# Two neighbouring products of a stencil made by one VectorE instruction, in five of ten steps

## The chip, the cores and the metric

The kernel runs on one core of a Trainium2 chip. The metric is the device time of one execution in microseconds (us); the median of three runs is given. A profile of one execution comes with it: when each instruction ran on each engine, what it waited for, and the clock that TensorE was granted.

## The reference, cut to what matters

Two layers are computed on an image batch of 8 x 32 x 32 pixels (H and W) and 64 channels. The second (a ternary 3x3 convolution) comes after the part that is changed. The first normalises the input, computes coefficient fields from convolutions and Sobel filters, and then takes five steps of a recurrence:

```python
K = 5
cm_x, cp_x = (-Ax + 2.0 * Bx, Ax + 2.0 * Bx)
cm_y, cp_y = (-Ay + 2.0 * By, Ay + 2.0 * By)
for _ in range(K):
    prev = h
    h = D * (c0 * h0 - 2.0 * E * h
             + cm_x * jnp.roll(h, 1, axis=2) + cp_x * jnp.roll(h, -1, axis=2)
             + cm_y * jnp.roll(h, 1, axis=3) + cp_y * jnp.roll(h, -1, axis=3))
    h = h + D * (2.0 * DT) * fsrc
    h0 = prev
```

Axis 2 is the position w in a row, axis 3 is the channel. So each step needs five products of a coefficient field with the present state (two of it shifted by one row position, two by one channel, one not shifted), one product with the state before it, and a source term.

## The kernel before, in words

The batch is cut into two tiles t = 0 and 1 of four images. A tile is 128 partitions (32 image rows by 4 images) by 2048 columns (32 positions w by 64 channels), all fp32. The five steps of the two tiles run interleaved: `ORDER` at line 38 is (0,0), (1,0), (0,1), (2,0), (1,1), (3,0), (2,1), (4,0), (3,1), (4,1), each a pair (k, t) of step and tile. Below, "step (2,0)" means step k = 2 of tile 0.

`coef` holds seven coefficient fields of each tile, 2048 columns each; A0, AE, FS, AXM, AXP, AYM and AYP are their numbers (AYM is 2 and AYP is 5). `state` holds for each tile two copies of h with a border of one position and one channel around it, so that a shifted h is a view that begins elsewhere (`h_at`).

One step (k, t) is this work:

- VectorE (`step`, lines 978 to 1005, and `multiply`, lines 906 to 919) makes the five products in the order AYP, AXP, AE, AXM, AYM. Each is one instruction of 2048 columns, and each writes one of three slots of a buffer `ring` in turn. A product may start when the slot's former content has been summed: the semaphore wait in `wait_summed` asks for all products up to the third last one. `product` is counted up by one at its end.
- In the five steps (1,0), (2,0), (1,1), (3,0) and (2,1) VectorE then makes a sixth product of the same length, A0 times h, into `first_two` (line 1004), which is kept for the tile's next step. GpSimd's queue then adds the source to it by an accumulating DMA (line 350).
- TensorE (`add_source`, `back_to_natural`, `add_products`, the loop at line 1306) sums in PSUM. Each summand takes 16 transposing matmuls of 128 x 128 (line 1180). For a step it first sums the kept product of that tile, then turns the state of the step before back to natural layout (line 1087, 16 matmuls), then sums the five products as they come. So 7 groups of 16 matmuls belong to a step.
- ScalarE (line 380) copies the finished sum from PSUM, copies what TensorE turned back into `state`, and fills the border (four small copies). The next step of the same tile waits for that border. Between two steps of one tile there is a step of the other tile, except for (1,0), which comes right behind (0,0), and (4,1), right behind (3,1).

The order on each engine is the order of the code; there is no scheduler. VectorE makes the last coefficient fields of tile 1 between step (0,0) and step (1,0).

Of the kernel before, what the change touches and what calls it, by code (L numbers as in the profile page):

```python
# [9 lines left out]

# [1 line left out]

# [1 line left out]

B, H, W, C = 8, 32, 32, 64
TILES = 2
# [8 lines left out]
STEPS = 5  # L25
# [8 lines left out]
A0, AE, FS, AXM, AXP, AYM, AYP = 1, 6, 0, 3, 4, 2, 5  # L34
RING = 3
# [39 lines left out]
def network(nc, x, wide_taps, norms, matrices, out_cols, conv_w, out):  # L75
    f32, f32r, i32 = mybir.dt.float32, mybir.dt.float32r, mybir.dt.int32
    ALU, ACT, AX = mybir.AluOpType, mybir.ActivationFunctionType, mybir.AxisListType

    jobs = job_table()
    job_no = {name: i for i, (name, _) in enumerate(jobs)}  # L80
    slot_of = dict(jobs)
    uses_before, seen = {}, [0] * SLOTS
# [4 lines left out]
    with ExitStack() as ctx:  # L87
        def sb(name, shape, dt=f32):
            return ctx.enter_context(nc.sbuf_tensor(name, shape, dt))

        def sem(name):
            return ctx.enter_context(nc.semaphore(name))


        coef = sb("coef", [128, TILES, NCOEF, N])
        state = sb("state", [128, TILES, 2, ROWS, PITCH])
        ring = sb("ring", [128, RING, N])
# [57 lines left out]
        def h_at(t, k, dw=0, dc=0, w0=0, w1=W):  # L155

            return state[:, t, k % 2, 1 + dw + w0:1 + dw + w1, 1 + dc:1 + dc + C]
# [7 lines left out]
        def wc(ap):  # L165
            return ap.rearrange("p (w c) -> p w c", c=C)

        def half(ap, h):
            return ap[:, h * HALF:(h + 1) * HALF]
# [8 lines left out]
        def part(ap, t, i):  # L178
            return ap[:, out_cuts[t][i]:out_cuts[t][i + 1]]
# [16 lines left out]
        def slot_ap(name):  # L196
            return psum[:, slot_of[name], :]
# [17 lines left out]
        newton_ready, axp_ready, ayp_ready = sem("newton_ready"), sem("axp_ready"), sem("ayp_ready")  # L215
# [3 lines left out]
        ax_full, ay_full = ([sem(f"{n}{t}") for t in range(TILES)] for n in ("ax_full", "ay_full"))  # L219
# [7 lines left out]
        product, ring_free = sem("product"), sem("ring_free")  # L227
# [11 lines left out]
        def wait_job(eng, name):  # L239

            eng.wait_ge(pe_job, job_no[name] + 1)

        def wait_reader(eng, name):

            eng.wait_ge(slot_free[slot_of[name]], uses_before[name] + 1)

        def frees(ins, name):
            ins.then_inc(slot_free[slot_of[name]], 1)

        def kept(k, t):  # L250

            return k > 1 and (k, t) != ORDER[-1]
# [9 lines left out]
        def states_through(k, t):  # L262

            return sum(kk < STEPS - 1 for kk, _ in ORDER[:ORDER.index((k, t)) + 1])
# [365 lines left out]
        def _(dve):  # L630
            steps, asked = [0], [0]
            V = nc.vector
# [262 lines left out]
            made = [0]  # L895
            sum_ends = {products_through(k, t): (k, t) for k in range(STEPS) for t in range(TILES)}

            def wait_summed(n):

                if n in sum_ends:  # L900
                    k, t = sum_ends[n]
                    wait_job(dve, f"acc_{k}_{t}_1")
                else:
                    dve.wait_ge(ring_free, n - sum(end < n for end in sum_ends))

            def multiply(t, k, a, dw, dc):

                slot = made[0] % RING
                if made[0] < 2:
                    wait_job(dve, "t2_1_1")  # L910
                    dve.wait_ge(ayp_ready, 1)
                    dve.wait_ge(ae_ready, 1)
                if made[0] == 2:
                    dve.wait_ge(dense_m_ready, 6)
                if made[0] >= RING:
                    wait_summed(made[0] - RING + 1)
                made[0] += 1
                V.tensor_tensor(wc(ring[:, slot, :]), wc(coef[:, t, a, :]), h_at(t, k, dw, dc), ALU.mult)\  # L918
                    .then_inc(product, 1)

            def residual(t):

                for h in range(2):
                    wait_reader(dve, f"acc_{STEPS - 1}_{t}_{h}")
                    wait_job(dve, f"tx_{t}_{h}")
                    frees(V.tensor_tensor(half(coef[:, t, 2, :], h), slot_ap(f"tx_{t}_{h}"),
                                          half(coef[:, t, 0, :], h), ALU.add), f"tx_{t}_{h}")
                    wait_reader(dve, f"tx_{t}_{h}")
                    x1 = half(coef[:, t, 2, :], h).rearrange("p (j h b) -> p j h b", b=BT, h=H)
                    for b in range(0, BT, 2):  # L930
                        V.bn_stats(stats[:, t, h, b:b + 2, :].rearrange("p b s -> p (b s)"), x1[:, :, :, b:b + 2])\
                            .then_inc(mv_ready, 1)
# [40 lines left out]
            def output_sum(t, h):  # L973
                wait_reader(dve, f"cf_{t}_{h}")
                V.tensor_tensor(part(coef[:, t, 3, :], t, h), part(coef[:, t, 0, :], t, h),  # L975
                                part(coef[:, t, 2, :], t, h), ALU.add).then_inc(sum_ready, 1)

            def step(k, t, then_do=()):

                def then(i):  # L980
                    for at, what in then_do:
                        if at == i:
                            what()

                if k > 1 and not kept(k, t):
                    multiply(t, k + 1, A0, 0, 0)
                then(-1)
                if k == 0:
                    dve.wait_ge(s_halo, 4 * (t + 1))
                else:  # L990
                    dve.wait_ge(halo_ready, 4 * states_through(k - 1, t))
                for i, (a, dw, dc) in enumerate(((AYP, 0, 1), (AXP, 1, 0), (AE, 0, 0), (AXM, -1, 0), (AYM, 0, -1))):
                    if k == 0 and i == 0:
                        dve.wait_ge(ayp_ready, t + 1)
                        dve.wait_ge(axp_ready, t + 1)
                    if k == 0 and a == AXM:
                        dve.wait_ge(ax_full[t], 16)
                    if k == 0 and a == AYM:
                        dve.wait_ge(ay_full[t], 16)
                    multiply(t, k, a, dw, dc)  # L1000
                    then(i)
                if k and k + 1 < STEPS and kept(k + 1, t):
                    dve.wait_ge(kept_free[t], k)
                    V.tensor_tensor(wc(first_two[t][:, :]), wc(coef[:, t, A0, :]), h_at(t, k), ALU.mult)\  # L1004
                        .then_inc(kept_made[t], 1)
# [37 lines left out]
            then(V.tensor_tensor(outw[:, 1:2], outw[:, 2:3], outp[:, 2:3], ALU.mult))  # L1043
            signal(V.tensor_tensor(outw[:, 3:4], outp[:, 1:2], outw[:, 1:2], ALU.add), outw_ready, 1)
            step(0, 0)
            over_rows(1)
            over_channels(1)
            divergence_taken()
            source(1)
            step(1, 0)  # L1050
            for k, t in ORDER[2:-1]:
                step(k, t)
            residual(0)
            step(STEPS - 1, 1, ((-1, lambda: spread(0)), (0, lambda: ask_norm(0)), (1, lambda: second_norm(0)),
                                  (3, lambda: normalise(0))))
            lower_half(0, 0)
            lower_half(0, 1)
            residual(1)
            spread(1)
            ask_norm(1)  # L1060
# [350 lines left out]
```

## Time and profile before

| what | us |
|---|---|
| median of three runs (lowest, highest) | 279.26 (278.02, 279.52) |
| the profiled execution, device time | 277.91 |
| its span, from first to last instruction | 276.1 |
| TensorE busy | 233.6 (85% of the span) |
| VectorE busy | 247.2 (90%) |
| ScalarE busy | 133.8 (48%) |

The profiled execution took 1.35 us less than the median of the three runs. In a row of a timeline the first number is the start in us from the begin of the span, the second how long the group took, then engine, line, operation, what was written and read, the count (x5), and in brackets how long the engine had been idle before and which engine ended that. PE is TensorE, PEld its weight loads, DVE VectorE, ACT ScalarE, POOL GpSimd.

### The profile page before, as it was taken

What the parts mean: (1) busy time and instruction counts of PE and PEld (TensorE: products, weight loads), DVE (VectorE), ACT (ScalarE), POOL (GpSimd) and SP (SyncE); (2) the same over time, 40 slices, a digit from 0 to 9 for tenths busy, and PEclk for the clock granted to TensorE, in tenths of its full rate; (3) what the DMA queues carried; (4) which work ended last, traced back from release to release, by engine and by line L of the source; (5) the groups of instructions that cost most, each with busy time, mean ns of one, the idle gap of its engine ahead of it and who ended that gap; (6) DMA issues with size and microseconds to landing.
All of it is one profiled execution on the core that took longest, in us unless ns stands there. A gap on an engine that the chain in (4) does not pass through costs nothing.

```text
span 276.1 us, 5235 instructions
## 1 busy us (share of the span) xinstructions
PE 233.6 (85%) x2276; PEld 209.6 (76%) x2276; DVE 247.2 (90%) x196; ACT 133.8 (48%) x207; POOL 16.8 (6%) x36
## 2 busy tenths in 40 slices
PE   0137999999959999279999999999999987889793
PEld 0136889989925588279989999898989986767683
DVE  3799999999999989999998999999999989886821
ACT  3294776879860054702623425160603246917743
POOL 2000000003310201101000101010101000000000
PEclk9999999999979999959999999999999999999999
DMA  6950000005998771990700334248610030000124
GB/s 213 350 116 0 0 4 6 2 0 112 199 205 253 152 152 38 209 209 2 154 0 2 76 78 94 61 116 190 129 26 1 0 138 17 2 0 0 62 93 152
DMA packets 7190, 24.94 MB, mean 90 GB/s; under 512 B 2816, under 2 KB 3328, under 8 KB 5120
## 3 DMA queue, kind: packets, MB, share of 16 engines
q0 software_dynamic: 2304, 14.68, 26.6%
q1 hardware_dynamic: 4720, 9.61, 10.6%
q10 hardware_dynamic: 144, 0.33, 0.4%
q8 instruction: 18, 0.29, 0.4%
q14 instruction: 4, 0.03, 0.0%
HBM read 6.79 MB, written 2.10 MB: 32 GB/s over the span
## 4 chain that ended last, share of the span: by engine, by line
DVE 54%; PE 27%; issue 9%; ACT 7%; DMA 1%; DVEq 0%; ACTq 0%
DVE ring L918 24%; DVE coef L653 8%; PE psum L1180 8%; PE psum L1170 6%; ACT coef L380 5%; PE psum L1257 5%; DVE first_two L1004 4%; PE psum L1117 3%; PE psum L1087 3%; DVE state L729 2%; DVE coef L964 1%; DMA bn<-in_norms 1%; DVE ring L722 1%; DVE hi_s L734 1%; DVE gsum L687 1%
## 5 line engine op out<-in xcount | busy, mean ns | idle before, releaser
L918 DVE TENSOR_TENSOR ring<-coef,state 128x2048 f32<-128x2048 f32 x51 | 113.5, 2286 | 2.1 <-PE psum L1180 1.9
L1180 PE MATMUL psum<-mats,ring 128*128 128x128 f32 x816 | 96.6, 278 | 9.6 <-DVE ring L918 9.5
L1180 PEld LDWEIGHTS psum<-mats,ring 128*128 128x128 f32 x816 | 91.4, 144 | 13.3 <-DVE ring L918 12.9
L380 ACT ACTIVATE state<-psum 128x1024 f32<-128x1024 f32 x36 | 35.1, 1028 | 74.3 <-PE psum L1180 60.2
L653 DVE SCALAR_TENSOR_TENSOR coef<-coef 128x2048 f32<-128x2048 f32 x16 | 36.4, 2290 | 0.7 <-issue 0.2
L380 ACT ACTIVATE coef<-coef 128x2048 f32<-128x2048 f32 (+1 forms) x10 | 17.6, 1783 | 10.1 <-DMA coef<-coef 9.9
L1257 PE MATMUL psum<-hi,dense_m 128*128 128x512 f32 (+1 forms) x54 | 20.0, 379 | 0.9 <-ACT coef L380 0.9
L1139 PEld LDWEIGHTS psum<-coef,state 32*128 32x128 f32 x672 | 19.4, 187 | 1.4 <-issue 1.3
L380 ACT ACTIVATE coef<-psum 128x512 f32<-128x512 f32 (+2 forms) x23 | 17.5, 766 | 5.4 <-PE psum L1117 4.3
L1139 PE MATMUL psum<-coef,state 32*128 32x64 f32 x672 | 20.0, 271 | 0.0
L1257 PE MATMUL psum<-lo,dense_m 128*128 128x512 f32 (+1 forms) x54 | 19.5, 369 | 0.0
L1180 PE MATMUL psum<-mats,first_two 128*128 128x128 f32 x144 | 17.3, 273 | 1.8 <-issue 1.2
L1180 PEld LDWEIGHTS psum<-mats,first_two 128*128 128x128 f32 x144 | 15.9, 141 | 2.3 <-ACT state L380 1.4
L1087 PE MATMUL psum<-mats,state 128*128 128x128 f32 x128 | 15.4, 273 | 0.7 <-ACT state L380 0.7
L1087 PEld LDWEIGHTS psum<-mats,state 128*128 128x128 f32 x128 | 14.1, 141 | 1.2 <-ACT state L380 1.1
L380 ACT ACTIVATE coef<-coef,gn 64x512 f32<-64x512 f32 x9 | 11.3, 1322 | 3.4 <-DVE gn L653 3.4
L975 DVE TENSOR_TENSOR coef<-coef 128x512 f32<-128x512 f32 (+2 forms) x7 | 5.4, 767 | 8.2 <-ACT coef L380 8.1
L1117 PE MATMUL psum<-hi_s,sobel_m 128*128 128x512 f32 (+2 forms) x48 | 12.1, 391 | 0.2 <-DVE hi_s L734 0.2
L1170 PE MATMUL psum<-coef,mats 128*128 128x512 f32 (+2 forms) x20 | 9.6, 616 | 3.1 <-ACT first_two L380 3.1
L1257 PEld LDWEIGHTS psum<-hi,dense_m 128*128 128x128 f32 x54 | 10.2, 188 | 2.7 <-issue 1.1
L380 ACT ACTIVATE coef<-psum,outp,wred 128x512 f32<-128x512 f32 (+2 forms) x7 | 5.9, 838 | 13.0 <-PE psum L1257 13.0
L1270 PE MATMUL psum<-gsum,mats 128*128 128x32 f32 x4 | 1.2, 404 | 12.2 <-DVE gsum L687 12.2
(133 smaller groups left out, 280.4 us busy)
## 6 DMA issues: line engine op xcount, KB each, us to landing
first_two<-coef POOLq DMA_DIRECT2D x7, 1024.0 KB, 8.5
coef<-coef POOLq DMA_DIRECT2D x5, 1024.0 KB, 8.8
coef<-in_x SPq DMA_DIRECT2D x2, 1024.0 KB, 6.0
coef<-in_wide_taps SPq DMA_DIRECT2D x3, 384.0 KB, 7.6
ring<-in_x SPq DMA_DIRECT2D x2, 512.0 KB, 6.0
ring<-in_x SPq DMA_DIRECT2D x1, 1024.0 KB, 10.3
coef<-coef SPq DMA_DIRECT2D x1, 1024.0 KB, 7.6
out<-coef SPq DMA_DIRECT2D x2, 512.0 KB, 3.1
```

Source lines behind the costliest of these rows:

```text
L380: return nc.scalar.activation(dst, src, func, **kw)
L653: return V.scalar_tensor_tensor(out=out_ap, in0=in0, scalar=scalar, in1=in1, op0=op0, op1=op1)
L729: signal(V.tensor_tensor(s, s, root(t).unsqueeze(1).broadcast_to([128, W, C]), ALU.mult), s_ready, t + 1)
L918: V.tensor_tensor(wc(ring[:, slot, :]), wc(coef[:, t, a, :]), h_at(t, k, dw, dc), ALU.mult)\
L975: V.tensor_tensor(part(coef[:, t, 3, :], t, h), part(coef[:, t, 0, :], t, h), part(coef[:, t, 2, :], t, h), ALU.add).then_inc(sum_ready, 1)
L1004: V.tensor_tensor(wc(first_two[t][:, :]), wc(coef[:, t, A0, :]), h_at(t, k), ALU.mult)\
L1087: ins = nc.tensor.transpose(dst[:, j * 128:j * 128 + 128], src, ident)
L1117: ins = mm(dst[:, bank * BANK + to * C:bank * BANK + (to + count) * C], sobel_m[:, m, :], part[:, frm * C:(frm + count) * C], start=(i == ...
L1139: ins = mm(banks[a][:, j * 2 * W:(j + 1) * 2 * W], sT[t][p, 8 * h + j, dy * BT:dy * BT + 128], taps(8 * h + j)[p, dy, :, :].rearrange("p v ...
L1170: ins = mm(out_ap, m, src, start=(i == 0), stop=(i == len(pieces) - 1), skip_group_check=True)
L1180: ins = mm(slot_ap(name)[:, (j % 8) * 128:(j % 8) * 128 + 128], src[:, j * 128:j * 128 + 128], ident, is_transpose=True, start=first and j ...
L1257: ins = mm(to, dense_m[:, b, dy, :], rows[:, j0 + b:j1 + b, dy * BT:dy * BT + 128], start=(n == 0), stop=(n == len(steps) - 1))
```

## The change

In the five steps that keep a product, the two products of the channel direction (AYM with the state one channel lower, AYP with the state one channel higher) become one instruction of 4096 columns, and it stands first in the step. The two coefficient fields are read with a stride of three fields, the two shifted states as one view with a step of two elements between its halves, and two slots of `ring` are written: slots 0 and 1, or 1 and 2, or 2 and 0, as they come. It waits until all but the last product before it have been summed, and counts `product` up by two at its end. The other three products and the kept one follow. The other five steps are as before; their code is moved into a function of its own.

```diff
+            def multiply_both_channels(t, k):
+
+                slot = made[0] % RING
+                wait_summed(made[0] - RING + 2)
+                made[0] += 2
+                to = ring[:, slot:slot + 2, :] if slot + 2 <= RING else ring[:, 0:RING:RING - 1, :]
+                factors = coef[:, t, AYM:AYP + 1:AYP - AYM, :]
+                left = h_at(t, k, 0, -1)
+                both = bass.AP(left.tensor, left.offset, [left.ap[0], [2, 2], *left.ap[1:]])
+                V.tensor_tensor(to.rearrange("p k (w c) -> p k w c", c=C),
+                                factors.rearrange("p k (w c) -> p k w c", c=C), both, ALU.mult).then_inc(product, 2)
...
+                if k and k + 1 < STEPS and kept(k + 1, t):
+                    multiply_both_channels(t, k)
+                    for a, dw, dc in ((AXP, 1, 0), (AE, 0, 0), (AXM, -1, 0)):
+                        multiply(t, k, a, dw, dc)
+                else:
+                    single_products(t, k, then)
```

On VectorE, at steps (1,0), (0,1) and (2,0), this stands in a row before the change (`ring_free` and `pe_job` count what TensorE has summed, `halo_ready` the borders of the state, `kept_free` the reading of the kept product):

```order
L653 SCALAR_TENSOR_TENSOR coef<-coef,state 128x2048 [waits slot_free3,slot_free2]
L918 TENSOR_TENSOR ring<-coef,state 128x2048 [waits ring_free,halo_ready]
L918 TENSOR_TENSOR ring<-coef,state 128x2048 [waits ring_free]
L918 TENSOR_TENSOR ring<-coef,state 128x2048 [waits pe_job]
L918 TENSOR_TENSOR ring<-coef,state 128x2048 [waits ring_free] x2
L1004 TENSOR_TENSOR first_two0<-coef,state 128x2048 [waits kept_free0]
```

and this with the change, at the same place:

```order
L653 SCALAR_TENSOR_TENSOR coef<-coef,state 128x2048 [waits slot_free3,slot_free2]
L930 TENSOR_TENSOR ring<-coef,state 128x2x2048 [waits ring_free,halo_ready]
L918 TENSOR_TENSOR ring<-coef,state 128x2048 [waits pe_job]
L918 TENSOR_TENSOR ring<-coef,state 128x2048 [waits ring_free] x2
L1025 TENSOR_TENSOR first_two0<-coef,state 128x2048 [waits kept_free0]
```

Six instructions have become five; the first one now holds two products, and the product behind it waits for the whole sum of the step before (`pe_job`), as the third did.

On VectorE again, step (2,0) and the start of step (1,1), as a difference:

```order
-L918 TENSOR_TENSOR ring<-coef,state 128x2048 [waits ring_free,halo_ready]
-L918 TENSOR_TENSOR ring<-coef,state 128x2048 [waits ring_free]
+L930 TENSOR_TENSOR ring<-coef,state 128x4096 [waits ring_free,halo_ready]
 L918 TENSOR_TENSOR ring<-coef,state 128x2048 [waits pe_job]
 L918 TENSOR_TENSOR ring<-coef,state 128x2048 [waits ring_free] x2
-L1004 TENSOR_TENSOR first_two0<-coef,state 128x2048 [waits kept_free0]
-L918 TENSOR_TENSOR ring<-coef,state 128x2048 [waits ring_free,halo_ready]
-L918 TENSOR_TENSOR ring<-coef,state 128x2048 [waits ring_free]
+L1025 TENSOR_TENSOR first_two0<-coef,state 128x2048 [waits kept_free0]
+L930 TENSOR_TENSOR ring<-coef,state 128x2x2048 [waits ring_free,halo_ready]
```

The same happens in each of the five steps; TensorE's, ScalarE's and GpSimd's instructions keep their order.

## Rows read from the trace of the kernel before

**Rows 1.** The page: busy time by engine, and the granted clock in 40 slices
```profile
PE 233.6 (85%) x2276; PEld 209.6 (76%) x2276; DVE 247.2 (90%) x196; ACT 133.8 (48%) x207; POOL 16.8 (6%) x36
PEclk9999999999979999959999999999999999999999
```
**Rows 2.** Timeline of VectorE from 111 to 216 us
```profile
111.96 2.35 DVE L885 TENSOR_TENSOR coef<-psum,coef 128x1024 f32<-128x1024 f32 x2
114.41 2.29 DVE L653 SCALAR_TENSOR_TENSOR coef<-coef,state 128x2048 f32<-128x2048 f32 x1
116.62 11.09 DVE L918 TENSOR_TENSOR ring<-coef,state 128x2048 f32<-128x2048 f32 x5
...
148.23 4.50 DVE L918 TENSOR_TENSOR ring<-coef,state 128x2048 f32<-128x2048 f32 x2 [0.69 <-PE psum L1180]
...
154.84 11.09 DVE L918 TENSOR_TENSOR ring<-coef,state 128x2048 f32<-128x2048 f32 x5
165.85 2.28 DVE L1004 TENSOR_TENSOR first_two<-coef,state 128x2048 f32<-128x2048 f32 x1
168.06 11.09 DVE L918 TENSOR_TENSOR ring<-coef,state 128x2048 f32<-128x2048 f32 x5
```
**Rows 3.** The chain that ended last: start us, us, what; 194 to 219 us
```profile
194.57 8.69 DVE ring L918 x4
203.29 2.29 DVE ring L918
205.63 7.20 PE psum L1180 x64
212.84 1.75 PE psum L1087 x16
214.58 4.38 PE psum L1180 x40
218.99 1.03 ACT state L380
```
**Rows 4.** VectorE durations, ns least/median/greatest of a line; then two timeline rows of shorter ones
```profile
L918 DVE TENSOR_TENSOR ring<-coef,state x51: 2274/2285/2295, 90.6 to 236.6; 128x2048 f32<-128x2048 f32 x51
L722 DVE TENSOR_TENSOR ring<-state,gsum x2: 2292/2294/2295, 19.9 to 37.9; 128x2048 f32<-128x2048 f32 x2
255.53 1.23 DVE L975 TENSOR_TENSOR coef<-coef 128x1024 f32<-128x1024 f32 x1
...
264.37 0.69 DVE L975 TENSOR_TENSOR coef<-coef 128x512 f32<-128x512 f32 x1 [2.08 <-ACT coef L380]
```
**Rows 5.** Timeline of TensorE from 78 to 180 us
```profile
79.20 3.62 PE L1170 MATMUL psum<-coef,mats 128*128 128x512 f32 x6 [3.12 <-ACT first_two L380]
...
111.46 1.94 PE L1180 MATMUL psum<-mats,first_two 128*128 128x128 f32 x16 [1.17 <-issue]
118.96 11.09 PE L1180 MATMUL psum<-mats,ring 128*128 128x128 f32 x80 [5.57 <-DVE ring L918]
129.89 1.91 PE L1180 MATMUL psum<-mats,first_two 128*128 128x128 f32 x16
...
133.38 7.37 PE L1180 MATMUL psum<-mats,ring 128*128 128x128 f32 x64
140.99 1.97 PE L1180 MATMUL psum<-mats,ring 128*128 128x128 f32 x16 [0.23 <-DVE ring L918]
...
146.28 8.90 PE L1180 MATMUL psum<-mats,ring 128*128 128x128 f32 x80
155.01 1.91 PE L1180 MATMUL psum<-mats,first_two 128*128 128x128 f32 x16
156.76 1.91 PE L1087 MATMUL psum<-mats,state 128*128 128x128 f32 x16
158.51 7.25 PE L1180 MATMUL psum<-mats,ring 128*128 128x128 f32 x64
165.99 1.97 PE L1180 MATMUL psum<-mats,ring 128*128 128x128 f32 x16 [0.24 <-DVE ring L918]
167.79 1.91 PE L1180 MATMUL psum<-mats,first_two 128*128 128x128 f32 x16
```
**Rows 6.** Windows: from:to us, length, PE busy (matmuls), granted clock, DMA share, GB/s
```profile
79.00:79.50 0.50, 0.30 (x1) 0.51 0.96 190
82.00:82.50 0.50, 0.50 (x2) 0.57 0.95 186
82.50:83.00 0.50, 0.50 (x4) 1.00 0.97 198
...
116.00:116.50 0.50, 0.00 (x0) 1.00 1.20 246
116.50:117.00 0.50, 0.00 (x0) 0.56 0.95 197
...
123.00:123.50 0.50, 0.50 (x5) 0.61 1.20 246
```
**Rows 7.** The stretch 150 to 205 us: ScalarE's border copies before step (2,1)
```profile
172.65 0.71 ACT L380 ACTIVATE state<-state 128x64 f32<-128x64 f32 x4
181.27 11.09 DVE L918 TENSOR_TENSOR ring<-coef,state 128x2048 f32<-128x2048 f32 x5
```

More of the change, by code:

```diff
@@ L11 @@
 from contextlib import ExitStack
-from concourse import mybir
+from concourse import bass, mybir
 B, H, W, C = 8, 32, 32, 64
@@ L976, in output_sum, with single_products @@
                                 part(coef[:, t, 2, :], t, h), ALU.add).then_inc(sum_ready, 1)
+            def single_products(t, k, then):
+                for i, (a, dw, dc) in enumerate(((AYP, 0, 1), (AXP, 1, 0), (AE, 0, 0), (AXM, -1, 0), (AYM, 0, -1))):
+                    if k == 0 and i == 0:
+                        dve.wait_ge(ayp_ready, t + 1)
+                        dve.wait_ge(axp_ready, t + 1)
+                    if k == 0 and a == AXM:
+                        dve.wait_ge(ax_full[t], 16)
+                    if k == 0 and a == AYM:
+                        dve.wait_ge(ay_full[t], 16)
+                    multiply(t, k, a, dw, dc)
+                    then(i)
             def step(k, t, then_do=()):
@@ L991, in step @@
                     dve.wait_ge(halo_ready, 4 * states_through(k - 1, t))
[L992 to L1001, printed above, removed]
+                if k and k + 1 < STEPS and kept(k + 1, t):
+                    multiply_both_channels(t, k)
+                    for a, dw, dc in ((AXP, 1, 0), (AE, 0, 0), (AXM, -1, 0)):
+                        multiply(t, k, a, dw, dc)
+                else:
+                    single_products(t, k, then)
                 if k and k + 1 < STEPS and kept(k + 1, t):
```

## The prediction

> **What bounds the kernel now.** I read the page first: VectorE and TensorE are both busy nearly all the time [rows 1], so neither share says which one sets the end. The timeline of VectorE says it for the stretch that is changed. From 154.84 us on, steps follow each other with no idle time: 154.84 to 168.06 is 13.22 us for six instructions of 2048 columns, 2.20 us from start to start [rows 2]. TensorE has seven groups of 16 matmuls in the same step. A group takes 156.76 - 155.01 = 1.75 us, seven take 12.25, and it waits about 1 us in a step for a product [rows 5]. So VectorE bounds here, with TensorE close behind. The chain that ended last agrees: it runs along VectorE's products up to 205.6 us, and along TensorE from there [rows 3]. All of what happens between 116 and 205 us therefore arrives at the end one for one.
>
> Ahead of 154.84 the roles are different. VectorE waits once, 0.69 us, at 148.23 [rows 2]: the fourth product of step (2,0) needs the slot of the first, and TensorE began to sum that one only at 146.28 [rows 5]. TensorE is late there because of what happened at 118.96. It had been idle for 5.57 us, until the first product of step (1,0) was done [rows 5]. The granted clock had fallen from full (2.4 GHz) to half (1.2 GHz) between 116.5 and 117 and came back to full at about 123.4 [rows 6], the one dip that the page shows there [rows 1]. The 80 matmuls of the step took 129.89 - 118.96 = 10.93 us, against 155.01 - 146.28 = 8.73 us for the 80 of step (2,0) at full clock: 2.20 us lost. That fits half of the 4.4 us between the restart and the return of the clock. No product was missing meanwhile: the fifth was done at 116.62 + 11.09 = 127.71. So from 118.96 to 138.6 TensorE is the one that everything hangs on.
>
> **What the change saves on VectorE.** A 2048-column product takes 2.285 us and starts 2.20 us after the one before, since its start overlaps the other's end by 0.08 [rows 2, 4]. The 4096-column instruction is not in the trace. By the slope between 512 columns (0.69) and 2048 (2.285), 1.038 ns a column, it takes 2.285 + 2.13 = 4.41; by the slope from 1024 columns (1.23), 1.030 ns, 4.395. I take 4.41, the longer base line. From start to start that is 4.33 against 4.405 for two: 0.07 us saved in a step. The bounds: two full durations (4.57, a loss of 0.09), and 4.395 (a gain of 0.09). The pattern, three levels and a view that overlaps itself, should not slow it: a product with broadcast and regrouped operands at L722 takes 2.294 [rows 4]. In five steps 0.35, if all counted; those of (1,0) and (2,0) lie before the wait for TensorE at 148.23, which swallows them. Three are left: 0.21 us (bounds -0.27 and 0.27).
>
> A rule bears on this size. The trace shows successive products 2.20 us apart although each lasts 2.285. The Trainium skill, "VectorE: DVE Perf Modes", section "The TRN2 errata", gives fp32 tensor_tensor of N columns as (N + 151) / 0.96 ns and says that small tiles pay the fixed part each. By it two products cost 4.58 and the long one 4.42, 0.16 us a step, an estimate from that page; over three steps the saving would be 0.47 instead of 0.21 and the forecast 0.26 us lower. The trace speaks against counting it so, since most of the fixed part is overlapped.
>
> **What the change costs at step (1,0).** The first product no longer ends after 2.3 us but only with the second. The instruction starts at 116.62 as before, as the instructions ahead of it are untouched [rows 2]; it ends at 121.03 and TensorE restarts at 121.08 (0.05 us after, as at 118.96), 2.12 us later. The clock has fallen by then, at 116.5 to 117, before either restart [rows 6]. The question is when it comes back. The trace has two restarts at half clock: at 79.20 us it was back at 82.4, 3.2 us after; at 118.96 at 123.4, 4.4 us after [rows 5, 6]. I take the middle, 3.8 us, so a loss of 1.9. The 80 matmuls then end at 121.08 + 8.73 + 1.90 = 131.71, against 129.89: 1.82 us later. The later products are there in time (the fifth at 116.62 + 4.33 + 3 x 2.20 + 0.08 = 127.63), so nothing else delays it.
>
> How much of the 1.82 arrives: in step (0,1) TensorE waits for products. From 133.38 four sums of 1.75 would end at 140.36, the fifth begins at 140.99 [rows 5]: 0.63 us of slack. Behind it there is none up to 146.28. So the first sum of step (2,0) begins 1.82 - 0.63 = 1.19 us later, at 147.47, and VectorE's fourth product, which waits for it, starts 1.19 later as well, at 149.42. From there VectorE runs without a wait. The long instruction of step (2,0) itself is hidden: it starts once the fourth sum of (0,1) is done, some 142.4, and ends at 146.8, before TensorE asks for it.
>
> The Trainium skill, "TensorE: Matmul & The Clock Gate", section "What's actually happening", says that the throttled state is the default and that activity releases it. The fall during the idle stretch and the return after the restart agree with it [rows 5, 6]; it gives no reason that the return should stay at 123.4.
>
> **The later four steps.** In steps (1,1), (3,0) and (2,1) TensorE gets its first product at T + 4.46 (T being the step's start on VectorE) where it would be ready at about T + 3.6 (158.51 - 154.84 = 3.67). It idles some 0.8 us, but then has two products at once. Its seven groups (12.25) fit into VectorE's 13.15. The tightest wait is that of VectorE's product behind the pair and one more: free at T + 4.33 + 2.20 = 6.53, and it needs the first sum, which is done 1.95 us after its start (148.23 - 146.28 [rows 2, 5]), at T + 6.41. Margin 0.12 us, so I count nothing; the next one has 0.6. The finished sum comes at about T + 13.2, some 0.25 later than now; the border for the tile's next step was there at 173.36 for a step that begins at 181.27 [rows 7], 7.9 us of cover.
>
> **The sum.** Cost 1.19, saving 0.21: 0.98, say 1.0 us slower. Against the profiled execution (277.91) that is 278.9. The median of the runs shown is 1.35 us above that execution, so the expected median is 279.26 + 1.0 = 280.3 us, slower by 0.36%.
>
> **The rivals.** (a) The clock comes back no later than before, at 123.4. The loss is then (123.4 - 121.08) / 2 = 1.16, TensorE ends 121.08 + 8.73 + 1.16 = 130.97, 1.08 late; 0.45 arrives, less 0.21: 0.24 us slower, 279.5. For it speaks that the second restart's return took longer than the first's, so the return isn't a fixed time after the restart. Chance 0.2. (b) On the other side: the half clock doesn't matter, because the clock is full again soon after the restart or hasn't fallen. Full at the restart, the matmuls end at 121.08 + 8.73 = 129.81, earlier than now. The saving stands in four steps, 0.28 us: 279.0, faster. The cost is below the saving when TensorE ends less than 0.63 + 0.28 = 0.9 us late, that is with a loss under 1.0, when the clock is back within 2.0 us; neither restart in the trace shows that. Chance 0.1. (c) The return takes longer, or the 0.12 us of margin is not there. If the clock returns 5.5 us after the restart, TensorE ends 0.85 later than forecast: +1.8 us. If the fourth product waits 0.3 us in each of three steps (the bound is TensorE's present slack of 1 us a step, less what it must wait), +0.9 as well: 281.2. For it speaks that TensorE stands idle 7.7 us instead of 5.57, and has work for 12.25 of the 13.15 us of a step; against it, that 1.95 us is one measured number and the other rows give the same 0.05 from product to sum. Chance 0.15. The forecast has 0.55.
>
> **How the numbers follow.** 0.5% is 1.4 us, about what a measurement of this kernel can tell from no change. The forecast's own range, with returns of 3.2 and 4.4 us (losses 1.6 and 2.2: 0.7 and 1.3 us) and the bounds of the long instruction, is +0.5 to +1.6. The range over all takes in (a) and most of (b) and (c): -0.2 to +2.2, and some 0.4 for where a median falls in runs that lie 1.5 us apart: 278.7 to 281.8. Slower by over 0.5% takes most of (c) and a fifth of the forecast: 0.26. Faster by over 0.5% is no case here, only scatter: 0.03. The rest, 0.71, is within.
>
> **What would show it.** In the profile after: the long instruction at 4.41 us, and 13.15 us per step; TensorE's restart at 121.1, half clock behind it for over 2.5 us, and the 80 matmuls of step (1,0) ending near 131.7; VectorE's wait at step (2,0) grown, with its next step (1,1) starting near 156.0 instead of 154.84. I am wrong if VectorE starts step (1,1) at or before 154.9, if the long instruction takes over 4.6, or if VectorE waits in steps (1,1) to (2,1).

## The result, and the profile after

| | median us | lowest, highest | runs |
|---|---|---|---|
| before | 278.62 | 277.82, 279.52 | 17 |
| after | 279.90 | 279.27, 280.62 | 17 |

The changed kernel takes 1.0047 times the time of the one before (95% interval 1.0033 to 1.0060), 1.3 us more. The forecast was 1.0 us more. With more runs the median of before lies 0.64 us lower than the three runs gave, so the absolute time came out at 279.9 and not at 280.3.

The profiled execution of after took 280.57 us, its span 278.8. The page's lines that answer to [rows 1]:

```profile
PE 233.2 (84%) x2276; PEld 209.6 (75%) x2276; DVE 247.0 (89%) x191; ACT 133.9 (48%) x207; POOL 16.8 (6%) x36
...
PEclk9999999999969999959999999999999999999999
```

The busy times are those of before to within 0.4 us; VectorE has five instructions fewer. So the difference is idle time. The timeline of VectorE after the change, in the same columns as [rows 2]:

```profile
115.69 2.29 DVE L653 SCALAR_TENSOR_TENSOR coef<-coef,state 128x2048 f32<-128x2048 f32 x1
117.90 4.42 DVE L930 TENSOR_TENSOR ring<-coef,state 128x4096 f32<-128x4096 f32 x1
122.23 2.28 DVE L918 TENSOR_TENSOR ring<-coef,state 128x2048 f32<-128x2048 f32 x1
126.08 4.50 DVE L918 TENSOR_TENSOR ring<-coef,state 128x2048 f32<-128x2048 f32 x2 [1.57 <-PE psum L1201]
130.49 2.29 DVE L1025 TENSOR_TENSOR first_two<-coef,state 128x2048 f32<-128x2048 f32 x1
132.69 11.10 DVE L918 TENSOR_TENSOR ring<-coef,state 128x2048 f32<-128x2048 f32 x5
143.74 4.43 DVE L930 TENSOR_TENSOR ring<-coef,state 128x4096 f32<-128x4096 f32 x1
148.08 2.29 DVE L918 TENSOR_TENSOR ring<-coef,state 128x2048 f32<-128x2048 f32 x1
151.09 4.50 DVE L918 TENSOR_TENSOR ring<-coef,state 128x2048 f32<-128x2048 f32 x2 [0.72 <-PE psum L1201]
...
157.70 4.42 DVE L930 TENSOR_TENSOR ring<-coef,state 128x4096 f32<-128x4096 f32 x1
...
197.14 22.11 DVE L918 TENSOR_TENSOR ring<-coef,state 128x2048 f32<-128x2048 f32 x10
```

The reader is to see three stretches here:

- **Up to the start of step (1,0)**, 117.90 against 116.62 [rows 2]: 1.28 us later, and nothing in it was changed. TensorE's clock was at half until 85.0 us here (the window below), and until 82.4 in the execution of before [rows 6]. This is scatter between executions: in nine profiles that run the same code up to here, the start of step (1,0) follows that return of the clock (shown with the experiment that fills an earlier gap).
- **From (1,0) to (1,1)**: 157.70 - 117.90 = 39.80 us, against 154.84 - 116.62 = 38.22 before. This is the cost, 1.58 us. VectorE waits 1.57 us at the fourth product of step (1,0), where it did not wait before. The wait at step (2,0) is what it was (0.72 for 0.69).
- **From (1,1) to (4,0)**, three steps: 197.14 - 157.70 = 39.44 us. Before, step (4,0) began at 194.49 (the next timeline), so 39.65: 0.21 us are saved, as forecast.

```profile
194.49 22.10 DVE L918 TENSOR_TENSOR ring<-coef,state 128x2048 f32<-128x2048 f32 x10
```

1.28 + 1.58 - 0.21 = 2.65, the 2.7 us between the two spans. TensorE in the same stretch, timeline first, then windows in the columns of [rows 6]:

```profile
111.87 1.94 PE L1201 MATMUL psum<-mats,first_two 128*128 128x128 f32 x16 [1.16 <-issue]
122.37 10.68 PE L1201 MATMUL psum<-mats,ring 128*128 128x128 f32 x80 [8.56 <-DVE ring L930]
132.88 1.91 PE L1201 MATMUL psum<-mats,first_two 128*128 128x128 f32 x16
...
162.18 8.95 PE L1201 MATMUL psum<-mats,ring 128*128 128x128 f32 x80 [0.65 <-DVE ring L930]
```
```profile
119.00:119.50 0.50, 0.00 (x0) 0.62 0.56 115
...
125.50:126.00 0.50, 0.50 (x4) 0.55 0.12 16
84.50:85.00 0.50, 0.50 (x4) 0.51 0.71 147
```

TensorE restarts 4.47 us after VectorE began the step (122.37), with the clock at half, and the clock is full again at about 125.95, 3.6 us later. The chain that ended last shows how that gets back to VectorE:

```profile
117.90 4.43 DVE ring L930
122.32 0.04 issue
122.37 3.69 PE psum L1201 x16
126.06 0.02 issue
126.08 1.80 DVE ring L918
```

The first sum (the 16 matmuls of the first product) takes 3.69 us at half clock; at full clock it is 1.95, with its last matmul's latency (148.23 - 146.28 [rows 2, 5]). VectorE's fourth product writes the ring slot that this sum reads, and can't start before the sum has ended.

### The profile page after: what moved, and what is told of

Its sections match the earlier page's. It is cut to its first block, busy times and chain, and to the rows that moved or that the text cites. A ratio compares the mean times of both kernels' runs of the same rounds, so it can differ in the third digit from the quotient of the medians.

```text
span 278.8 us, 5230 instructions
## 1 busy us (share of the span) xinstructions
PE 233.2 (84%) x2276; PEld 209.6 (75%) x2276; DVE 247.0 (89%) x191; ACT 133.9 (48%) x207; POOL 16.8 (6%) x36
## 4 chain that ended last, share of the span: by engine, by line
DVE 56%; PE 28%; issue 10%; ACT 4%; DMA 1%; DVEq 0%; ACTq 0%
DVE ring L918 20%; PE psum L1201 10%; DVE coef L653 8%; PE psum L1191 7%; DVE ring L930 6%; PE psum L1278 5%; PE psum L1108 3%; DVE first_two L1025 2%; PE psum L1138 2%; ACT coef L380 2%; DVE coef L976 2%; DVE lo_s L737 2%; DVE state L729 2%; DMA bn<-in_norms 1%; DVE ring L722 1%
## 5 line engine op out<-in xcount | busy, mean ns | idle before, releaser
L1201 PE MATMUL psum<-mats,ring 128*128 128x128 f32 x816 | 94.8, 276 | 13.2 <-DVE ring L930 10.6
L918 DVE TENSOR_TENSOR ring<-coef,state 128x2048 f32<-128x2048 f32 x41 | 91.7, 2287 | 4.9 <-PE psum L1201 4.7
L930 DVE TENSOR_TENSOR ring<-coef,state 128x4096 f32<-128x4096 f32 x5 | 22.1, 4420 | 0.0
```

The lines of the kernel that those rows point to most:

```text
L930: V.tensor_tensor(to.rearrange("p k (w c) -> p k w c", c=C), factors.rearrange("p k (w c) -> p k w c", c=C), both, ALU.mult).then_inc(prod ...
L1201: ins = mm(slot_ap(name)[:, (j % 8) * 128:(j % 8) * 128 + 128], src[:, j * 128:j * 128 + 128], ident, is_transpose=True, start=first and j ...
```

## The experiments

Theory A, after the result: the whole cost arises in step (1,0). TensorE gets its first product 2.13 us later (4.47 us after the step's start instead of 2.34), still at half clock; the first sum ends so late that VectorE waits for its slot. Rivals: the long instruction costs a little wherever it stands (B), the instruction itself is slow (C), three slots are too few for two products at once, at any clock (D), or TensorE's own chain of sums sets the cost, as I had predicted (E). All ratios are against before, measured along with each kernel.

### The long instruction in four steps, not in (1,0)

```diff
-                if k and k + 1 < STEPS and kept(k + 1, t):
+                if k and k + 1 < STEPS and kept(k + 1, t) and (k, t) != (1, 0):
                     multiply_both_channels(t, k)
```

> The long instruction in (2,0), (1,1), (3,0) and (2,1), and two single products in (1,0) as before. Theory A: the whole cost arises in step (1,0), where VectorE's fourth product waits 1.57 us for a first sum that TensorE makes at half clock. Then there is no wait of VectorE in (1,0), the wait in (2,0) is near 0.7 as before, and the kernel is 0.2 to 0.3 us faster than before (ratio 0.999). Theory B: each long instruction costs something by holding back products. Then it stays 0.5 us or more slower than before (ratio 1.002 or more).

Measured: 278.37 us, ratio 0.9992 (0.9979 to 1.0006). VectorE's timeline:

```profile
117.38 11.09 DVE L918 TENSOR_TENSOR ring<-coef,state 128x2048 f32<-128x2048 f32 x5
...
148.98 4.50 DVE L918 TENSOR_TENSOR ring<-coef,state 128x2048 f32<-128x2048 f32 x2 [0.53 <-PE psum L1201]
...
155.60 4.42 DVE L930 TENSOR_TENSOR ring<-coef,state 128x4096 f32<-128x4096 f32 x1
```

From (1,0) to (1,1) it is 38.22 us again, to the hundredth. The three later steps take 39.43 (step (4,0) begins at 195.03). The cost is gone, so B falls; the gain of 0.2 us stands in the trace but is too small for the interval.

### The long instruction in (1,0) alone

```diff
-                if k and k + 1 < STEPS and kept(k + 1, t):
+                if (k, t) == (1, 0):
                     multiply_both_channels(t, k)
```

> The long instruction in step (1,0) alone. Theory A: slower than before by 1.3 to 1.6 us (ratio 1.005), with VectorE's wait of about 1.6 us at the fourth product of (1,0). Theory B: a fifth of the cost, 0.3 us (ratio 1.001).

Measured: 280.15 us, ratio 1.0057 (1.0037 to 1.0076). VectorE waits 1.39 us at the fourth product and needs 39.63 us from (1,0) to (1,1), where one step has the whole cost:

```profile
125.37 4.49 DVE L918 TENSOR_TENSOR ring<-coef,state 128x2048 f32<-128x2048 f32 x2 [1.39 <-PE psum L1201]
...
156.99 11.09 DVE L918 TENSOR_TENSOR ring<-coef,state 128x2048 f32<-128x2048 f32 x5
```

### No long instruction, but its first product withheld

```diff
-                V.tensor_tensor(wc(ring[:, slot, :]), wc(coef[:, t, a, :]), h_at(t, k, dw, dc), ALU.mult)\
-                    .then_inc(product, 1)
+                ins = V.tensor_tensor(wc(ring[:, slot, :]), wc(coef[:, t, a, :]), h_at(t, k, dw, dc), ALU.mult)
+                if (t, k, a) != (0, 1, AYP):
+                    ins.then_inc(product, 2 if (t, k, a) == (0, 1, AXP) else 1)
```

> The kernel before, with its ten instructions as they were; only the first product of step (1,0) does not tell TensorE that it is done, and the second counts two. Theory A: what costs is that TensorE gets its first product 2.2 us later, not the instruction: slower than before by 1.3 to 1.7 us (ratio 1.005), with the same wait at the fourth product. Theory C: it is the 4096-column instruction, by its length or its pattern: no change (ratio 1.000).

Measured: 279.99 us, ratio 1.0064 (1.0039 to 1.0088); one of its six runs took 281.56, the others 279.5 to 280.2. The kernel before, with only two semaphore counts changed, has the cost as soon as TensorE learns of the first product together with the second:

```profile
116.97 6.69 DVE L918 TENSOR_TENSOR ring<-coef,state 128x2048 f32<-128x2048 f32 x3
124.83 4.49 DVE L918 TENSOR_TENSOR ring<-coef,state 128x2048 f32<-128x2048 f32 x2 [1.16 <-PE psum L1181]
```

C falls. What costs is the grain of the hand-over, not the 4096-column instruction, which is 4.33 us from its start to the next one's where two single ones need 4.41. That TensorE's first product comes late is not enough by itself, as the next experiments show: the clock has to be at half, too. And the half clock alone, with the first product in time, costs nothing between (1,0) and (1,1): in the profile with the long instruction in four steps, the clock came back 5.2 us after TensorE's restart, and the stretch took 38.22 us all the same.

### The changed kernel with TensorE kept busy ahead of (1,0)

```diff
                 add_source(t, k)
+                if (k, t) == (1, 0):
+                    take_sums(1, 0)
+                    for j in range(56):
+                        mm(slot_ap("acc_0_1_0")[:, (j % 8) * 128:(j % 8) * 128 + 128], ident, ident,
+                           is_transpose=True, start=True, stop=True, skip_group_check=True)
```

> The changed kernel, with 56 matmuls of no use (identity turned into a PSUM slot that is free and is written anew afterwards) on TensorE behind the kept product of step (1,0), so that TensorE works for some 6.1 us of the 7.7 it stood idle. Nothing of the computation is left out. Theory A: the clock is full when the first product comes, the first sum takes 1.75 us and not 3.5, VectorE does not wait in (1,0), and the kernel is 0.2 to 0.3 us faster than before (ratio 0.999). Theory D: the three slots of the ring alone make VectorE wait once two products come at once, at any clock: slower than before by 1 us or more (ratio 1.004).

Measured: 278.37 us, ratio 1.0001 (0.9980 to 1.0022). Three of the twelve runs took 280.0 and the other nine 277.8 to 278.8. The profiled execution is one of the three. The matmuls of no use began 2 us late, since their slot had to be read first, and the clock fell 0.1 us behind their start:

```profile
115.82 7.97 PE L1342 MATMUL psum<-mats 128*128 128x128 f32 x56 [1.93 <-DVE coef L885]
123.63 8.90 PE L1201 MATMUL psum<-mats,ring 128*128 128x128 f32 x80
```

They took 7.97 us instead of some 6.2, so that TensorE came to its first product (ready at 122.41) 1.2 us late; VectorE waited 0.96 us and needed 39.21 us from (1,0) to (1,1). The rest of this run's length lies ahead of the changed code: its step (1,0) began at 117.99, 1.37 us later than in the profile of before. The nine faster runs were not profiled; their mean granted clock is 0.985 to 0.990, against 0.978 in the three. In the same kernel with 30 of the matmuls:

> As warm, but 30 useless matmuls instead of 56. In warm's profile the clock fell before they began, so that 56 of them took 7.97 us and TensorE came to the first product 1.2 us late; 3 of its 12 runs took 280.0 us and the others about 278.2. Theory A: 30 of them take 3.3 us at full clock and 6.4 at half and are done in time either way; no run is slowed as those three were, and the median is at or up to 0.3 us below before (ratio 0.999). Rival: TensorE stands idle again behind them for up to 3 us, the clock falls, and part of the wait in (1,0) is back: 0.3 to 0.8 us slower than before (ratio 1.002).

Measured: 279.94 us, ratio 1.0054 (1.0035 to 1.0074): mostly the rival's case, and larger than it said. Nine of the ten runs took 279.2 to 280.5, one took 277.44. That one is the profiled one, and it is what shows the mechanism cleanest:

```profile
116.46 4.42 DVE L930 TENSOR_TENSOR ring<-coef,state 128x4096 f32<-128x4096 f32 x1
120.80 6.69 DVE L918 TENSOR_TENSOR ring<-coef,state 128x2048 f32<-128x2048 f32 x3
...
154.62 4.42 DVE L930 TENSOR_TENSOR ring<-coef,state 128x4096 f32<-128x4096 f32 x1
```
```profile
114.29 3.47 PE L1342 MATMUL psum<-mats 128*128 128x128 f32 x30 [0.97 <-DVE coef L885]
120.94 8.96 PE L1201 MATMUL psum<-mats,ring 128*128 128x128 f32 x80 [3.18 <-DVE ring L930]
```

(VectorE first, then TensorE.) Here the clock stayed full, the 80 matmuls took 8.8 us, as at full clock before, and VectorE does not wait in (1,0) at all: 38.16 us to step (1,1), 0.06 less than before. The ring of three slots is enough for two products at once at full clock, so D falls, by this one profile. That the other nine runs had the half clock again is likely from their times and from their mean granted clock (0.975 to 0.982, against 0.990 in the profiled one), but they were not profiled.

### The kept product ahead of the last two

```diff
                     for a, dw, dc in ((AXP, 1, 0), (AE, 0, 0), (AXM, -1, 0)):
+                        if (k, t, a) == (1, 0, AE):
+                            keep()
                         multiply(t, k, a, dw, dc)
```

(`keep()` is the wait for `kept_free` and the A0 product of the kernel, left out at its old place in this step.)

> The changed kernel, but in step (1,0) the kept product (A0 times h, into first_two) is made as the third instruction, ahead of the two last products. So the fourth product comes 2.2 us later, at a time when the first sum is done even at half clock. Theory A, that VectorE's wait in (1,0) is the way by which the cost arrives: no wait there, and only what TensorE's own chain passes on is left (about 1.7 us late at the end of the step's sums, less 0.63 us of slack in step (0,1)): 0.7 to 1.0 us slower than before (ratio 1.003), 0.4 to 0.6 us better than the changed kernel. Theory E: TensorE's chain alone sets the cost, as the prediction had it, and the wait is only beside it: as slow as the changed kernel (ratio 1.0047).

Measured: 279.87 us, ratio 1.0046 (1.0030 to 1.0061). The number is E's, against my expectation. The trace shows why it does not decide (VectorE, TensorE and a window of the clock):

```profile
125.16 11.10 DVE L918 TENSOR_TENSOR ring<-coef,state 128x2048 f32<-128x2048 f32 x5
137.87 4.49 DVE L918 TENSOR_TENSOR ring<-coef,state 128x2048 f32<-128x2048 f32 x2 [1.60 <-PE psum L1206]
143.14 4.43 DVE L930 TENSOR_TENSOR ring<-coef,state 128x4096 f32<-128x4096 f32 x1 [0.78 <-PE psum L1206]
```
```profile
120.90 11.62 PE L1206 MATMUL psum<-mats,ring 128*128 128x128 f32 x80 [7.49 <-DVE ring L930]
132.36 1.91 PE L1206 MATMUL psum<-mats,first_two 128*128 128x128 f32 x16
```
```profile
126.00:126.50 0.50, 0.50 (x5) 0.58 0.00 0
```

VectorE does not wait in (1,0) any more, as A said. But the clock came back 5.5 us after the restart in this execution, the 80 matmuls took 132.36 - 120.90 = 11.46 us, and TensorE's chain passes that on one step later, in (0,1) and (2,0). The step's sums end 15.94 us after the step began (at 116.42) instead of 13.27; 2.67 less the 0.63 us of slack is 2.04, and the trace has 40.22 - 38.22 = 2.00. So the prediction's sum is right for this kernel. There are two ways by which the late restart gets through: VectorE's wait in (1,0), at most 1.6 us and reached as soon as the whole first sum is at half clock, and TensorE's chain, which has no such limit but 0.63 us of slack. Taking the first way away leaves the second. How late the clock came back in the eleven runs without a profile is not known. With the changed kernel's 3.6 us the second way alone would give 1.08 us, 0.5 less than the first, and the median shows no such gain; so this experiment does not say by which way the cost arrives in the runs that were not profiled.

### A second profile of the changed kernel

> The changed kernel once more, for a second profile of it. Theory A: VectorE's wait at the fourth product of (1,0) follows the part of the first sum that runs at half clock: at most some 1.6 us, with the whole sum at half clock, however late the clock comes back; and VectorE's step (1,1) starts between 38.2 and 39.9 us after (1,0). The first profile had a wait of 1.57 and 39.80.

```profile
117.07 4.42 DVE L930 TENSOR_TENSOR ring<-coef,state 128x4096 f32<-128x4096 f32 x1
121.41 2.28 DVE L918 TENSOR_TENSOR ring<-coef,state 128x2048 f32<-128x2048 f32 x1
124.88 4.50 DVE L918 TENSOR_TENSOR ring<-coef,state 128x2048 f32<-128x2048 f32 x2 [1.19 <-PE psum L1201]
...
156.50 4.42 DVE L930 TENSOR_TENSOR ring<-coef,state 128x4096 f32<-128x4096 f32 x1
```

The execution took 279.62 us. Step (1,1) starts at 156.50, 39.43 us after (1,0). Together with the others, in us (the return of the clock is read from half-microsecond windows):

| kernel | first sum, with latency | clock back after the restart | VectorE's wait | (1,0) to (1,1) |
|---|---|---|---|---|
| held10 | 3.31 | 2.7 | 1.16 | 39.48 |
| after, second profile | 3.34 | 2.8 | 1.19 | 39.43 |
| only10 | 3.54 | 3.2 | 1.39 | 39.63 |
| after | 3.71 | 3.6 | 1.57 | 39.80 |
| warm30 | full clock | - | 0 | 38.16 |

(held10 and only10 name the two experiments with the withheld and the lone long instruction.) The wait follows the length of the first sum one for one, and the stretch to (1,1) with it. By E, TensorE's chain alone, the four kernels with a late return would lose what their 80 matmuls end later, less the slack: 14.64, 14.60, 14.80 and 14.98 us after the step's start in the order of the table, less 13.27 and 0.63, which is 0.74, 0.70, 0.90 and 1.08 us. They lose 1.26, 1.21, 1.41 and 1.58 against the 38.22 of before. So in these four profiles the wait is the way, and E falls for them; in the profile of the kernel with the kept product moved ahead it is E's way.

### TensorE kept busy in an earlier gap

The scatter ahead of step (1,0) asked for a test of its own. TensorE stands idle from 76.0 to 79.2 us, waiting for ScalarE to empty PSUM, and comes back at half clock [rows 5, 6]. In the nine profiles without matmuls of no use in this gap, the clock fell each time, in the gap or at most 0.4 us behind it, TensorE restarted between 79.1 and 79.6 us, and the clock was full again between 82.0 us (the kernel with the kept product moved) and 85.2 us (the one with 56 matmuls of no use). Step (1,0) then began between 116.42 and 117.99, in the same order but for two that lie 0.02 us apart: 1.57 us later for 3.16 us more of half clock. The first and the last of the nine, as windows:

```profile
82.00:82.50 0.50, 0.50 (x4) 0.96 1.02 201
```
```profile
85.00:85.50 0.50, 0.50 (x2) 0.80 0.87 180
```

The edit fills the gap:

```diff
             depthwise(1, 1)
+            wait_reader(pe, "cv_1_0")
+            for j in range(28):
+                mm(slot_ap("cv_1_0")[:, (j % 8) * 128:(j % 8) * 128 + 128], ident, ident,
+                   is_transpose=True, start=True, stop=True, skip_group_check=True)
             divergence(0)
```

> The kernel before, with 28 useless matmuls (identity into a PSUM slot that ScalarE has just emptied) between TensorE's depthwise sums and its divergence, where it stands idle from 76.0 to 79.2 us. Theory A, widened: the half clock behind that idle stretch (until 82.4 us in the profile of before, until 83.4 to 85.0 in five others) is paid in full, as the chain that ended last runs along TensorE there, and its length, not the same in each run, is why runs of one kernel lie 1.7 us apart. Then it is faster than before by 1 to 2.4 us (ratio 0.994) and its runs lie within 1 us. Rival F: VectorE or a DMA is next in line there: less than 0.5 us faster (ratio 0.999).

Measured: 276.53 us, ratio 0.9931 (0.9909 to 0.9952), and its six runs lie between 276.50 and 276.63, where the twenty of before lie between 277.59 and 279.52. TensorE and the windows:

```profile
76.11 3.28 PE L1305 MATMUL psum<-mats 128*128 128x128 f32 x28
79.25 2.02 PE L1170 MATMUL psum<-coef,mats 128*128 128x512 f32 x6
...
103.40 2.81 PE L1180 MATMUL psum<-mats,first_two 128*128 128x128 f32 x16 [3.07 <-DMA first_two<-coef]
```
```profile
76.00:80.00 4.00, 4.00 (x34) 1.00 1.05 211
112.00:118.00 6.00, 3.03 (x26) 1.00 0.98 198
```

The first six matmuls of the divergence take 2.02 us instead of 3.62 [rows 5]. The next limit follows some 20 us later: TensorE waits 3.07 us for a DMA, where it waited 0.65 before, so not all of the time gained arrives. VectorE's step (1,0) begins at 115.40, and from there to (1,1) it is 38.22 us as before; so the whole gain lies ahead of (1,0). Both with the long instruction in four steps:

> Both: the long instruction in four steps but not in (1,0), and the 28 useless matmuls of awake. The gains lie in different places and should add: awake's plus 0.2 us (ratio 0.9935). If the wait of VectorE for TensorE at step (2,0) swallowed one of them, it would be as awake.

Measured: 276.47 us, ratio 0.9930 (0.9908 to 0.9952), 0.06 us below the one without. Step (4,0) begins at 192.96 in its trace and at 193.26 in that of the kernel with the 28 matmuls alone, 0.1 us of which was there at step (1,0); the 0.2 us of the long instructions is there but not beyond what the medians can tell. Its six runs lie between 276.29 and 277.09. And with all five long instructions:

> The changed kernel, long instruction in all five steps, with the 28 useless matmuls of awake between depthwise and divergence. What it tells: whether the cost in step (1,0) is still there when the stretch before it is no longer disturbed. In awake's profile TensorE had its first product of (1,0) after 1.8 us of idleness and the clock stayed full; with the long instruction it stands idle some 2 us more, as long as in no10_awake (3.64 us), where the clock did fall. Theory A: if the clock falls, 1.2 to 1.6 us slower than no10_awake (276.5), so about 278 (ratio 0.998). If it stays full, as no10_awake: 276.3 (ratio 0.993).

Measured: 278.38 us, ratio 0.9996 (0.9981 to 1.0012), 1.9 us above the kernel with four of them. The idle stretch ahead of (1,0) cost the clock again; it fell at about 120.4, just behind TensorE's restart. TensorE and VectorE there:

```profile
120.01 10.62 PE L1201 MATMUL psum<-mats,ring 128*128 128x128 f32 x80 [4.09 <-DVE ring L930]
```
```profile
123.39 4.49 DVE L918 TENSOR_TENSOR ring<-coef,state 128x2048 f32<-128x2048 f32 x2 [1.23 <-PE psum L1201]
```

So one long instruction, the one in (1,0), undoes nearly all that the 28 matmuls bring. Its profiled execution, one of the fastest (277.89 us), shows 39.48 us from (1,0) to (1,1), 1.26 more than before; where the rest of the 1.9 us lies in the other runs, which range from 277.64 to 279.22, was not traced. With four of them the clock fell too in its profile, at about 118.2, but TensorE already had its first product, and the stretch took 38.23 us. The kernel with four long instructions and these matmuls is faster than both kernels of the case; nearly all of that is from the matmuls.

## Why the prediction was right, and where it was not

- **The bound.** Right. VectorE bounds from 154.84 us on, TensorE ahead of it, and what is lost there arrives in full: 1.28 + 1.58 - 0.21 explains the span.
- **The long instruction.** Forecast 4.41 us, measured 4.419 (4.417 to 4.426), and 13.15 us for a step (170.85 - 157.70). The saving of 0.21 us in three steps came out to the hundredth. The Trainium skill, "VectorE: DVE Perf Modes", section "The TRN2 errata", has (N + 151) / 0.96 ns, 4.424 for 4096 columns; the trace agrees with the duration. By that formula the fixed part is 0.157 us (an estimate from that page); merging two instructions saves only 0.07 of it here, since 0.08 is overlapped anyway.
- **The restart.** Right: 4.47 us after the step's start in both profiles of the changed kernel, at half clock, and the full clock did not come back at a fixed moment. I took 3.8 us for the return; the two profiles have 3.6 and 2.8, the others with a clock that had fallen before TensorE's restart 2.7 to 5.5. In the first profile the 80 matmuls ended 14.98 us after the start of the step, forecast 15.09.
- **How the delay arrives: wrong step, nearly right size.** I wrote that the later products are there in time, so nothing else delays it, and then that 0.63 of 1.82 us is absorbed in step (0,1). The fourth product was not in time. I had checked that wait in the later steps (margin 0.12 us, with a first sum of 1.95) but not in (1,0), where the first sum is at half clock and takes 3.7. VectorE is itself 1.57 us late from there, so TensorE's slack in (0,1) absorbs nothing. The term of 1.19 us measured 1.58 in the profile. With my own return of 3.8 us the same check would have given it: 4.46 + 3.69 - 6.53 = 1.62. So the sign that I named, a wait at step (2,0) grown, did not come (0.72 us for 0.69), and step (1,1) began at 157.70 instead of 156.0, 1.28 of it from the scatter ahead. That the way I left out gives 1.6 us and the way I took 1.2, so that the total came out nearly right, is luck. The second way is real, but it set the cost in one profile only, with the wait taken away and the latest return of all.
- **The later four steps.** Right: TensorE idles 0.65 to 0.70 us per step and VectorE never waits in (1,1), (3,0) and (2,1), on a margin of 0.12 us.
- **The rivals.** (a) The return at the old moment was not seen; it lies between 124.2 and 126.4 in the five profiles with a late restart and a fall before it. (b) A full clock, and with it a kernel no slower, occurred in one profiled execution, and only with added matmuls. (c) With a late first product, a return at over 5 us was seen once, and cost 2.0 us; the 0.12 us of margin held in both profiles. In the changed kernel it would have to go through TensorE's chain; whether some of its runs did is open. The 281.2 us in that rival is the forecast with the 0.9 us alone; with both of its parts the sum is 279.26 + 1.8 + 0.9 = 282.0, just outside the range that I gave.

## What to carry to other kernels

Merging two instructions saves only what is not overlapped already (0.07 us of 4.4 here), and it hands over two results at the time of the second. Where the consumer has been idle, that first hand-over is what ends its idleness; where it still has work, it cost nothing here. Even behind the gap it cost nothing in the one profile where TensorE's clock was full; late and at half clock together were what cost 1.2 to 1.6 us. So merge in the steady steps and keep the first step behind a gap fine-grained. And when a wait is checked for a margin, check it in the step with the slowest consumer, not in the steady one.

## What the runs showed of the hardware

TensorE's half clock after a gap was the larger matter in this kernel. Behind the idle stretch from 76 us the clock was at 1.2 GHz until anything from 82.0 to 85.2 us in nine profiles, and step (1,0) began up to 1.57 us later with it. That is of the size of the 1.9 us by which runs of one kernel lay apart. With the gap filled the six runs of one kernel lay within 0.13 us; but those of the kernel with four long instructions lay within 0.80, and with all five, where the clock falls again ahead of (1,0), the twelve runs lay within 1.58. So this gap is not the only source of scatter. The Trainium skill, "TensorE: Matmul & The Clock Gate", section "What's actually happening", calls the penalty less than 1% of a typical kernel's span. Filling this gap brought 0.7%, which agrees, and it was more than the change under study. Filling a gap needs care, though: the 56 matmuls of no use that met the half clock took 7.97 us instead of some 6.2 and made TensorE late in the one profiled run, and three of the twelve runs took 280.0 us; 30 of them leave 3.2 us of idleness behind them, and nine of ten runs were as slow as with none, likely for that reason.
